# Softmax attention on one core: scores ahead of the first half tile of transposes in each slot

## What is computed

```python
    x = x + 0.5 * _L0_ffn_ref(_layernorm(x, axis=-1), L0_ffn_weight, L0_ffn_bias)
    x = x + _L0_attn_ref(_layernorm(x, axis=-1), L0_attn_Wq, ...)
    x = x + 0.5 * _L0_ffn_ref(_layernorm(x, axis=-1), L0_ffn_weight, L0_ffn_bias)
    x = x + 0.5 * _L1_ffn_ref(_layernorm(x, axis=-1), L1_ffn_Wr, ...)
    x = x + _L1_attn_ref(_layernorm(x, axis=-1), L1_attn_w_qkv, L1_attn_w_out)
    x = x + 0.5 * _L1_ffn_ref(_layernorm(x, axis=-1), L1_ffn_Wr, ...)
...
        logits = jnp.einsum('bkpsd,bktd->bkpst', q, k) * scale
        attn = jax.nn.softmax(logits.astype(jnp.float32), axis=-1)
        combined = jnp.einsum('bkpst,bktd->bkpsd', attn, v.astype(jnp.float32)).astype(v.dtype)
        ...
        return combined @ w_out
```

## Time and profile before

| | |
|---|---|
| median of 3 runs | 3441.98 us (3441.32 to 3443.99) |
| the profiled execution's own time | 3439.03 us |
| its span | 3437.3 us |
| granted TensorE clock, mean | 0.993 |
| PE busy | 3336.6 us, 97% of the span |
| PE weight loads busy | 2854.1 us, 83% |
| DVE busy | 2671.8 us, 78% |
| ACT busy | 2042.7 us, 59% |
| POOL busy | 1059.2 us, 31% |

### The profile page before, as it was taken

The page is one execution under the profiler, slowest core; times in us unless marked ns, Lnnn a source line. Parts: engine busy times, 40 slices in busy tenths (PEclk is TensorE's granted clock), DMA queues, the critical chain, the costliest instruction groups (busy, mean ns, idle before and its releaser), DMA issues.

```text
span 3437.3 us, 53015 instructions
## 1 busy us (share of the span) xinstructions
PE 3336.6 (97%) x19523; PEld 2854.1 (83%) x19526; DVE 2671.8 (78%) x5155; ACT 2042.7 (59%) x3733; POOL 1059.2 (31%) x1293
## 2 busy tenths in 40 slices
PE   6899999999999999999999999999999999999997
PEld 4788888778888888888888888888888888888885
DVE  6899996778877778867888677886788767876776
ACT  4777777665556565555555656556555565556553
POOL 4887767522122122122121312212212121212112
PEclk9999999999999999999999999999999999999999
DMA  2222112200000000000000110000000010000000
GB/s 86 88 77 62 59 56 84 62 15 13 13 25 25 13 13 13 15 24 25 15 15 13 31 43 15 13 16 26 23 13 15 18 30 26 16 19 29 28 19 21
DMA packets 98528, 104.24 MB, mean 30 GB/s; under 512 B 10336, under 2 KB 88800, under 8 KB 98144
## 3 DMA queue, kind: packets, MB, share of 16 engines
q1 hardware_dynamic: 98272, 100.85, 9.7%
HBM read 87.18 MB, written 13.63 MB: 29 GB/s over the span
## 4 chain that ended last, share of the span: by engine, by line
PE 72%; DVE 5%; ACT 3%; issue 0%; POOL 0%; DVEq 0%; ACTq 0%; POOLq 0%
PE at_ps_job L2042 12%; PE at_ps_job L35 7%; PE at_ps_job L37 7%; PE at_ps_job L36 7%; PE at_ps_o L35 6%; PE at_ps_o L37 6%; PE at_ps_o L36 6%; PE at_ps_s L35 6%; PE at_ps_s L36 6%; PE at_ps_s L37 6%; DVE at_neg_max L1969 1%; ACT x_resident L1793 1%; DVE at_probT_lo L1836 1%; PE at_ps_job L656 1%; DVE li_wkv_lo L1867 0%; ACT at_probT_hi L1752 0%
## 5 line engine op out<-in xcount | busy, mean ns | idle before, releaser
L1752 ACT ACTIVATE at_probT_hi<-at_ps_job 128x512 fp32r<-128x512 f32 x1024 | 611.7, 598 | 889.1 <-PE at_ps_job L2042 886.8
L1836 DVE TENSOR_TENSOR at_probT_lo<-at_ps_job,at_probT_hi 128x512 fp32r<-128x512 f32 x1024 | 702.8, 686 | 273.0 <-ACT at_probT_hi L1752 262.5
L1793 ACT ACTIVATE x_resident<-at_ps_s,at_neg_max 128x1024 f32<-128x1024 f32 x512 | 570.9, 1115 | 149.5 <-DVE at_neg_max L1969 144.7
L1727 POOL TENSOR_TENSOR li_wkv_hi<-li_bkv,ch_cols 128x256 fp32r<-128x256 f32 x252 | 154.4, 613 | 1608.2 <-PE at_ps_job L37 1557.4
L1969 DVE TENSOR_REDUCE at_neg_max<-at_ps_s 128x1 f32<-128x1024 f32 x512 | 622.1, 1215 | 5.2
L2042 PE MATMUL at_ps_job<-ident,x_resident 128*128 128x128 f32 x4096 | 613.8, 272 | 4.7 <-DVE at_probT_lo L1836 3.0
L2042 PEld LDWEIGHTS at_ps_job<-ident,x_resident 128*128 128x128 f32 x4096 | 495.9, 140 | 97.6 <-issue 7.3
L35 PE MATMUL at_ps_o<-at_probT_hi,at_v_lo 128*128 128x512 f32 x1024 | 446.3, 436 | 7.5 <-DVE li_wkv_lo L1867 6.5
L35 PE MATMUL at_ps_s<-at_k_hi,at_q_lo 128*128 128x512 f32 x1024 | 445.1, 435 | 0.0
L37 PE MATMUL at_ps_o<-at_probT_lo,at_v_hi 128*128 128x512 f32 x1024 | 404.7, 395 | 0.0
L36 PE MATMUL at_ps_s<-at_k_hi,at_q_hi 128*128 128x512 f32 x1024 | 402.0, 393 | 0.0
(11 more groups left out here) (358 smaller groups left out, 7443.1 us busy)
## 6 DMA issues: line engine op xcount, KB each, us to landing
li_bkv<-attn_w SPq DMA_DIRECT2D x256, 128.0 KB, 2.3
li_bkv<-mlp_w SPq DMA_DIRECT2D x112, 128.0 KB, 2.3
li_wo_hi<-li_wo_kept SPq DMA_DIRECT2D x24, 256.0 KB, 2.6
li_wo_lo<-li_wo_kept SPq DMA_DIRECT2D x24, 256.0 KB, 3.0
li_wq_hi<-li_wq_kept SPq DMA_DIRECT2D x48, 128.0 KB, 2.1
li_wq_lo<-li_wq_kept SPq DMA_DIRECT2D x48, 128.0 KB, 2.3
x_resident<-x SPq DMA_DIRECT2D x4, 1024.0 KB, 12.7
out<-x_resident SPq DMA_DIRECT2D x4, 1024.0 KB, 4.9
```

Of the source, the lines that this page charges most:

```text
L1727: nc.gpsimd.tensor_tensor(hi, src, none, ALU.add).then_inc(s_wh[part], 1)
L1752: nc.scalar.activation(ph[:, i // TC, 4 * half:4 * half + 4, (i % TC) * P:(i % TC + 1) * P], c.turned_bank(2 * TB * u + 2 * i + half), ACT ...
L1793: nc.scalar.activation(prob[:, slot % 2, :], ps_s[slot % 2][:], ACT.Exp, bias=nmax[:, slot:slot + 1], accum_out=rsum[:, u % 2, slot:slot + ...
L1836: nc.vector.tensor_tensor(pl[at], c.turned_bank(2 * TB * u + 2 * i + half), ph[at].bitcast(F32), ALU.subtract).then_inc(s_pl, 1)
```

## The change

On PE, in every slot, the scores are issued ahead of T0 instead of behind it. Nothing else is edited: the same instructions, the same banks, the same order on ACT, DVE, POOL and SP.

```diff
@@ -2076,14 +2076,14 @@
                 u, slot = divmod(t, TB)
                 has_last, has_own = u >= 1, u < UNITS
                 turned = turned_tile(t)
+                if has_own:
+                    if TB * u + slot >= 2:
+                        pe.wait_ge(s_exp, TB * u + slot - 1)
+                    scores(u, slot)
                 if turned:
                     back, i = turned
                     pe.wait_ge(s_exp, TB * back + i + 1)
                     turn(back, i, 0)
-                if has_own:
-                    if TB * u + slot >= 2:
-                        pe.wait_ge(s_exp, TB * u + slot - 1)
-                    scores(u, slot)
                 values_part(u, slot, 0)
                 if turned:
                     turn(back, i, 1)
```

## The result

The change makes the kernel slower: 3542.12 us median (3539.91 to 3544.61, 4 runs) against 3441.65 us (3440.22 to 3443.99, 4 runs), a ratio of 1.0295 with a 95% interval of [1.0283, 1.0307]. The prediction was 3540 us. The profiled execution took 3544.61 us, with a span of 3542.9 us.

What follows compares the result with a forecast made beforehand. PE, busy 2626.78 of 2635 us in the softmax attention, sets the time. Terms 41 + 23 + 8 + 4 + 17 + 7 - 3 = 97 us gave 3539 against the median, stated as 3540; range 3490 to 3620.

Steps and rivals of the forecast that it cites:

- the late V's margin: Slot 498 before the change: late V's bank is free 1.1 us before Y, the slot's first job, takes it.
- The 7.2 us: PE's waits in the softmax attention before the change, in 17 places; no reordering of PE could win more.
- (a): First job waits for its bank until DVE has read out the late V: 94 x 0.44 = 41 us.
- (e): V0 of slots 2 and 6 waits for the attention output `out_low`, in odd units: 34 x 0.2 = 7 us.
- (b): First job waits for DVE's two-instruction readout of background jobs SC and QP: 36 x 0.63 = 23 us.
- (c): Waits for other background readouts: X and G 8 us, M2 4 us; R, T, M1, QT, read by ACT, 0.
- (d): PE's next job waits for ACT's gelus of HX, no margin left: 12 x 1.38 = 17 us.
- (f): T0's own waits on PE, 2.6 us, go away since T0 comes later: -3 us.
- PE's own work: 0: PE runs the same matmuls; transposes behind the scores instead of behind a job cost it nothing extra.
- What I gave as a sign: PE idle about 100 us; waits: L1862 90, L514/L488 36, L431 12, L1867 50; busy time moving over 10 us means transposes cost differently.
- The drain of 1.38 us: Skill rule for ACT's table load behind HX: 17 us more in 12 places; left out, as the trace disagreed.
- the swing: Rival: short idle moments make PE's clock fall to 0.94, adding 168 us, 3708 us in all; chance 0.02.

Runs made afterwards that it cites:

- e1: The change, with ACT and DVE reading out the last slot's late V and background job ahead of T0's high and low halves: 3455.4 us, ratio 1.0044.
- e5: Against the kernel before, T0 put between the two halves of the scores on PE: 3453.12 us, ratio 1.0039.
- e6: Against the kernel before, T0 put behind both the scores and V0 on PE: 3746.94 us, ratio 1.0897.
- e9: The change, with the late V alone read out ahead of T0's halves on ACT and DVE, background jobs staying behind: 3502.81 us, ratio 1.0183.
- e2: The change, with last slot's readouts ahead of T0's halves on ACT and DVE, and the maximum ahead of T0's low half: 3428.01 us, ratio 0.9965.
- e3: Against the kernel before, scores first only in slots that follow a slot with a late V, T0 first elsewhere: 3492.08 us, ratio 1.0152.
- e4: Against the kernel before, scores first only in slots following one without late V and without background job: 3453.94 us, ratio 1.004.

## Why the prediction was right

**The margin held; the bound was too low.** The waits that the change made are the ones named, and T0's delay and the late V's margin came out as read from slot 498: T0's low half starts at 2.64 in that slot (2.65 predicted) and the slot is 0.44 us longer (0.44 predicted). e1, e5, e6 and e9 show the mechanism apart from the total. The 7.2 us that were to be the most that a reordering can win are what the list shows of the old waits and not what they cost: e2 won 12 us, 9.4 of them in slots 9 to 509.

**The total was helped by luck.** 97 us predicted, 100.5 by the medians and 103.4 by the slots: (a) was sized too high and (e) too low by similar amounts, and they made up for each other.

**The terms.** (b), (c) for X, G and M2, and (d) came out within 1 us each. (a) was some 4 us too high: 87 of its 93 slots grew by 0.42 us on average, 36.9 in all. The other six became shorter, by 0.2 to 0.7 us, 2.6 in all: T0's own waits had stood there, three of about 0.3 us and three of 0.4, and they went. That is **(f)**, right in size too. e3 showed the other side of it, that these waits come back and grow when only the slots behind a late V have the new order.

The four kinds that ACT reads out grew by 2.5 us together, but not for a late readout: in e1 and e2, where the readouts come first, the same slots are 2.3 longer as well, each of the 12 behind an R by 0.11 in all three. R, T and QT are transposes, and the first score matmul behind transposes has its follower 0.31 us behind it in place of 0.23; before the change T0 stood between the two, and one such slow start did for both groups. So "PE's own work: 0" was wrong by 0.1 us in such slots, of which some of the slots ahead of them give back 0.08.

HX cost 1.47 us a slot and not 1.38. PE in the slot behind an HX job, the one of the earlier trace rows:

```profile
2004.72 0.48 PE L35 MATMUL at_ps_s<-at_k_hi,at_q_lo 128*128 128x512 f32 x1
...
2006.19 0.60 PE L2042 MATMUL at_ps_job<-ident,x_resident 128*128 128x128 f32 x4
...
2009.94 0.39 PE L35 MATMUL at_ps_job<-li_wkv_hi,li_wkv_lo 128*128 128x256 f32 x1 [1.31 <-ACT ch_r L431]
```

HX is itself a group of transposes, so the scores behind it have the slow first matmul (0.48), and T0 starts 2006.19 - 2004.72 = 1.47 into the slot.

**(e) was mis-sized: 14 us for 7.** I took 0.2 us in 34 slots, from slot 45. By the slots, 39 of the 48 grew, by 0.37 on average (14.4 us). The number of places was about right and the price too low, for three reasons. Of what slot 45 showed I had taken V0's late start, 0.28, and not the slower restart behind it, which I did count for the banks: in slot 46 V0's follower started 0.31 behind it, against 0.23 where V0 does not wait. The low half starts later than 2.65 in some of the slots ahead. And in 15 of the 39 DVE has an M2, QP or SC to read out between the low half and the maximum, which I had left out: these 15 grew by 0.44 each, the other 24 by 0.33, and the five of those with the low half at 2.63 to 2.66 and nothing else in the way by 0.28, which is my 0.2 and the restart (a sixth, slot 506, by 0.85; why is open). Slot 45 after the change, DVE:

```profile
913.32 0.68 DVE L1836 TENSOR_TENSOR at_probT_lo<-at_ps_job,at_probT_hi 128x512 fp32r<-128x512 f32 x1
...
916.89 0.69 DVE L1867 TENSOR_TENSOR li_wkv_lo<-at_ps_o,li_wkv_hi 128x512 fp32r<-128x512 f32 x1 [1.16 <-ACT li_wkv_hi L1771]
```

and PE, whose scores begin slot 45 at 910.52 and slot 46 at 915.58:

```profile
915.58 0.40 PE L35 MATMUL at_ps_s<-at_k_hi,at_q_lo 128*128 128x512 f32 x1
...
917.73 0.47 PE L35 MATMUL at_ps_o<-at_probT_hi,at_v_lo 128*128 128x512 f32 x1 [0.18 <-DVE li_wkv_lo L1867]
```

The low half starts at 2.80 and V0 at 2.15, where without a wait it stands 3410.26 - 3408.53 = 1.73 into the slot (slot 498). This is 0.42, and slot 46, which had paid nearly that before the change, grew by 0.04 only.

**What I gave as a sign was partly wrong.** The counts were: 90 waits for L1862, 36 for L514 and L488, 12 for L431, 32 (not 50) for L1867; and none for L1793 or L1836. But PE's idle time in the stretch grew to 61 us, not 100, and its busy time by 50, which by my own words would have meant that the transposes cost something else. They don't: in e2, where all slots have the new order, PE is busy 3328.3 us, 8 us less than before:

```profile
PE 3328.3 (97%) x19526; PEld 2837.2 (83%) x19526; DVE 2685.7 (78%) x5155; ACT 2056.3 (60%) x3733; POOL 1057.9 (31%) x1293
```

The 50 us are part of the waits. In slot 498 the wait cost 0.44 us and the list shows 0.17: the last matmul before it is drawn 0.40 long though its follower normally starts at 0.23, and the first one behind it 0.39 long in place of 0.28, with its follower 0.10 later. So this wait hides 0.27 us in busy time. It is not the same for every kind. A slot's growth less its listed wait, as the median of the slots with one wait and none before, is 0.26 for the late V, 0.27 for SC, 0.37 for QP, 0.33 for X, 0.24 for V0 and 0.16 for HX. M2's 24 slots, 0.18 us longer each, and G's 6, 0.31 each, have no wait in the list at all. In slots 9 to 509 together PE's idle time grew by 52.3 us and its busy time by 51.1.

**The rules weighed.** No drain is seen on either side of a table load with the change; ACT in that same slot, which answers to the earlier trace rows:

```profile
2006.83 0.60 ACT L1752 ACTIVATE at_probT_hi<-at_ps_job 128x512 fp32r<-128x512 f32 x1 [0.97 <-PE at_ps_job L2042]
2007.45 1.28 ACT L431 ACT_TABLE_LOAD   x1
2008.74 1.14 ACT L431 ACTIVATE ch_r<-at_ps_job,ch_b 128x128 f32<-128x128 f32 x4
```

The load starts 2007.45 - 2007.43 = 0.02 us behind the high half, and the gelu at 2008.74, 0.01 behind the load's end (2007.45 + 1.28). The drain of 1.38 us that the Trainium skill names (ScalarE: Activation LUTs, What ACT_TABLE_LOAD costs) would have made (d) about 17 us larger, and it was 17.6 in all. The granted clock stayed at 1.00 through the 182 listed stops of PE, and in e6 too, where PE was busy 2699.37 of 2940 us; of the swing that the Trainium skill describes (TensorE: Matmul & The Clock Gate, A second HAM failure mode) nothing shows here. PE's weight loads wait with the matmul, as in the earlier trace rows: at the late V's bank in slot 498 the load starts at 3412.51 and the matmul at 3412.52.

## What to carry to other kernels

When one engine is busy all the time, ask of a reordering not what it can win there but which margins it uses up: take one plain slot of the timeline, write down for each shared buffer when it is freed and when it is next claimed, and add the delay; a delay is free up to the margin and costs its full length times the number of places beyond it. A step that is moved on the producer wants its consumers' order moved with it: the same PE order costs 100 us with the old order on DVE and ACT, and wins 12 with theirs adapted (readouts of the last slot, the scores' maximum, then the transposes' half). Moving it in some slots only is to be checked for waits of its own: e3's mixture paid 14 us more than its slots' share, e4's nothing that shows.

## What was unexpected in the hardware's traces

A wait of PE costs more than the list of waits shows: 0.44 us against 0.17 in slot 498, and 0.16 to 0.37 us more by kind of wait. The smallest stops, 0.18 us in each of 24 slots behind M2, are not listed at all and show as busy time alone. Half of what the change costs stands in PE's busy time, though PE does no more work. A stall is then better measured by the distance of two starts that have the same work between them than by idle time.
